# A message pass over 400,000 edges: a ring of 13 chunks for 26, an earlier scatter, and TensorE picks in every second chunk

## What is computed

```python
h = jnp.maximum(_layernorm(x, axis=-1), 0.0)
x_i = h[dst]
x_j = h[src]
feat = jnp.concatenate([x_i, x_j - x_i], axis=-1)
m = jnp.maximum(feat @ W1 + b1, 0.0) @ W2 + b2
out = jax.ops.segment_max(m, dst, num_segments=N)
return x + jnp.where(jnp.isneginf(out), 0.0, out)
```

## Time and profile before

| | us |
|---|---|
| median of 3 runs (4907.32 to 4908.18) | 4908.1 |
| the profiled execution's own time | 4908.0 |
| its span | 4906.2 |
| busy in it: PE / PE's weight loads / DVE / ACT / POOL | 3227.3 / 1841.1 / 2427.4 / 893.1 / 3047.4 |
| the gathers of L386: number, busy | 2865, 2724.1 |
| the picks of L659: number recorded, busy | 9360, 2333.0 |

### The profile page before, as it was taken

One profiled execution on the slowest core, in us unless ns is written; L12 is line 12 of the kernel. 1 busy time (PEld: TensorE's weight loads), 2 busy tenths in 40 slices (PEclk: granted clock), 3 DMA queues, 4 the chain that ended last, 5 costly groups with the idle time before them and its releaser, 6 DMA issues.

```text
span 4906.2 us, 47353 instructions
## 1 busy us (share of the span) xinstructions
PE 3227.3 (66%) x14485; PEld 1841.1 (38%) x14745; DVE 2427.4 (49%) x7621; ACT 893.1 (18%) x3287; POOL 3047.4 (62%) x3186
## 2 busy tenths in 40 slices
PE   2100027777777777777777777777777777778960
PEld 2100004444444444444444444444444444444540
DVE  4100106555555555555555555555555555556861
ACT  4400202111111111111111111111111111112210
POOL 5677756666666666666666666666666666664017
PEclk8555558888888888888888888888888888888985
DMA  7866402222222222222222222222222222222222
GB/s 276 322 227 227 139 24 74 72 75 72 72 75 71 72 73 70 75 72 71 75 72 71 75 71 73 71 72 75 71 72 75 72 72 73 70 74 72 81 83 54
DMA packets 208533, 451.67 MB, mean 92 GB/s; under 512 B 61389, under 2 KB 64442, under 8 KB 207778
## 3 DMA queue, kind: packets, MB, share of 16 engines
q1 hardware_dynamic: 66703, 225.73, 14.3%
q0 software_dynamic: 103216, 117.29, 11.1%
q10 hardware_dynamic: 38362, 105.62, 5.9%
HBM read 230.84 MB, written 217.71 MB: 91 GB/s over the span
## 4 chain that ended last, share of the span: by engine, by line
another core or an unknown queue 41%; issue 28%; DVE 11%; ACT 9%; PE 6%; POOL 2%; DMA 1%; ACTq 1%; DVEq 0%; POOLq 0%; SPq 0%
ACT dst_all L535 5%; PE ps_g L659 5%; DVE state L896 4%; DVE a_fill L869 4%; POOL a_rows L443 2%; DVE rows L882 2%; ACT zt L547 1%; ACT dst_all L526 1%; ACTq L554 1%; DMA shared<-in_x_dram 1%; PE ps_m L678 1%; ACT zt L461 1%; ACT shared L568 0%; ACT shared L488 0%
## 5 line engine op out<-in xcount | busy, mean ns | idle before, releaser
L386 POOL DMA_INDIRECT rows<-b_table,src_idx x2865 | 2724.1, 951 | 1456.8 <-issue 804.3
L659 PE MATMUL ps_g<-shared,dst_all 128*128 128x512 bf16 x9360 | 2333.0, 403 | 255.7 <-issue 251.2
L659 PEld LDWEIGHTS ps_g<-shared,dst_all 128*128 128x128 bf16 x9620 | 1003.0, 105 | 1394.9 <-issue 509.7
L678 PE MATMUL ps_m<-w_diag,zt 128*128 128x128 f32 x3126 | 681.0, 399 | 726.0 <-ACT zt L547 722.5
L678 PEld LDWEIGHTS ps_m<-w_diag,zt 128*128 128x128 f32 x3126 | 611.1, 296 | 901.1 <-ACT zt L547 893.3
L896 DVE SCALAR_TENSOR_TENSOR state<-state,keep,ps_m 128x64 f32<-128x64 f32 x3125 | 859.8, 275 | 73.5 <-PE ps_m L678 43.1
L869 DVE SCALAR_TENSOR_TENSOR a_fill<-a_fill,keep 128x64 f32<-128x64 f32 x3125 | 874.0, 280 | 19.2
L924 DVE TENSOR_TENSOR dst_all<-ps_s,page_keys 128x1664 bf16<-128x1664 f32 x130 | 245.8, 1891 | 894.9 <-remote 890.4
L924 DVE TENSOR_TENSOR dst_all<-ps_x,page_keys 128x1664 bf16<-128x1664 f32 x130 | 245.8, 1891 | 847.9 <-remote 847.9
L547 ACT ACTIVATE zt<-ps_t 128x512 f32<-128x512 f32 (+1 forms) x521 | 226.6, 487 | 1688.6 <-remote 1656.4
L535 ACT ACTIVATE dst_all<-ps_g,dst_all 128x64 f32<-128x64 f32 x2080 | 454.7, 347 | 123.9 <-remote 80.5
(11 more groups left out here) (115 smaller groups left out, 556.2 us busy)
## 6 DMA issues: line engine op xcount, KB each, us to landing
a_edges<-state SPq DMA_DIRECT2D x80, 1250.0 KB
a_fill<-a_edges SPq DMA_DIRECT2D x260, 384.0 KB
states<-state ACTq DMA_DIRECT2D x260, 384.0 KB
rows<-b_table,src_idx POOLq DMA_INDIRECT x2865
shared<-in_x_dram SPq DMA_DIRECT2D x5, 625.0 KB
b_table<-shared ACTq DMA_DIRECT2D x5, 625.0 KB
a_table<-a_rows SPq DMA_DIRECT2D x1, 3125.0 KB
shared<-in_x_dram SPq DMA_DIRECT2D x1, 3125.0 KB
```

The lines of the kernel that those rows point to most:

```text
L386: nc.gpsimd.indirect_dma_start(out=rows[:, c % RING, t * C:(t + 1) * C], out_offset=None, in_=b_table, in_offset=at(src_idx[:, q % SRC_RIN ...
L659: last = nc.tensor.matmul(ps_g[:, half, :], key_is[:, half, g, :], table[:, g, t, :], start=(g, t) == (0, 0), stop=g == PAGES - 1)
L678: last = nc.tensor.matmul(ps_m[:, g, a * C:(a + m) * C], zt[0:m * C, g, a * C:a * C + P], w2_pair[0:m * C, 0:m * C], start=True, stop=True)
```

## The change

- The ring of `rows` has 13 chunks (RING). The search's blocks and the squares, which borrowed room in it, get tiles of their own.
- Picks are made only in chunks 4, 6, 8, ... 258 (EVERY, `picks_in`), 128 in all. The other 132 chunks gather all their 12 tiles. Keys, matches, picks, masks and sums are numbered by pick (`pick_number`) and left out in the other chunks. `gathered_count` gives the semaphore's value that a chunk's gathers end with.
- The 80 clears stand in a straight row and four are in flight (ZQ), each with its own semaphore.
- The store of a_table and the loads of the pages move from SP's queue to ACT's, the first two pages ahead of ACT's last `count_blocks`, the others each behind the split of the page two before.
- POOL gathers 10 chunks (PREFIX, 117 gathers) ahead of the scatters, not 25, and chunks 10 to 12 (34 gathers) behind them; the waits for z_turned begin with chunk 13.
- DVE's wait for the clears and the small gather stands behind the first matches instead of ahead of all of them. `first_dst` is a copy, so that the small gather doesn't read dst_all.
- ACT presets the maxima (one activation) behind step 5 instead of ahead of step 0.

The diff, cut to its core (asserts, new tiles and renamed arguments are left out):

```diff
-    RING = 26
+    RING = 13
...
+    ZQ = 4
...
-    GATHERED = CHUNK - 1
+    PRESET_AT = 5
+    PREFIX = 10
+    EVERY, FIRST_PICK = 2, PICK_AHEAD + 1
+
+    def picks_in(c):
+        return FIRST_PICK <= c < CHUNKS and (c - FIRST_PICK) % EVERY == 0
+
+    def pick_number(c):
+        return (c - FIRST_PICK) // EVERY
+
+    def picks_below(c):
+        return -(-max(0, min(c, CHUNKS) - FIRST_PICK) // EVERY)
+
+    def gathered_tiles(c):
+        return (CHUNK - 1 if picks_in(c) else CHUNK) if c < CHUNKS else TAIL
+
+    def gathered_count(c):
+        return 16 * sum(gathered_tiles(d) for d in range(c % RING, c + 1, RING))
...
+            for z in range(ZEROS):
+                if z >= ZQ:
+                    sp.wait_ge(zeros_stored[z % ZQ], 16 * (z // ZQ))
+                sp.dma_start(a_lanes[:, z * ZW * ZREP:(z + 1) * ZW * ZREP].rearrange("p (r w) -> p r w", w=ZW),
+                             zero_row).then_inc(zeros_stored[z % ZQ], 16)
...
-            def gather_chunk(c, tiles=GATHERED, done=None):
+            def gather_chunk(c, done=None):
                 q, j = divmod(c, BATCHED)
                 if j == 0:
                     pool.wait_ge(src_loaded[q % SRC_RING], (q // SRC_RING + 1) * 16)
-                for t in range(tiles):
+                for t in range(gathered_tiles(c)):
...
-            for c in range(RING - 1):
-                if c == BLOCKS_AT:
-                    pool.wait_ge(blk_used, SEARCHES)
+            for c in range(PREFIX):
                 gather_chunk(c)
             pool.wait_ge(scatter_ready, 1)
-            for half in range(2):
-                pool.wait_ge(zeros_stored[half], 16 * ZEROS // 2)
+            for s in range(ZQ):
+                pool.wait_ge(zeros_stored[s], 16 * ZEROS // ZQ)
...
             scatter_a(BATCH, NJ)
-            gather_chunk(RING - 1)
+            for c in range(PREFIX, RING):
+                gather_chunk(c)
             for c in range(RING, CHUNKS + 1):
                 pool.wait_ge(z_turned, (c - RING + 1) * GROUPS)
...
+            act.wait_ge(a_ready, NJ // 4)
+            act.dma_start(a_nodes, a_rows[0:NP, :, :]).then_inc(a_stored, 16)
+            act.wait_ge(b_stored, 16 * PIECES)
+            act.wait_ge(page_left, 1)
+            for g in range(2):
+                load_page(g)
             count_blocks(SEARCHES)
...
+                if g + 2 < PAGES:
+                    act.wait_ge(page_part, (g + 1) * PARTS)
+                    load_page(g + 2)
...
-                if c + KEYS_AHEAD < CHUNKS:
-                    spread_keys(c + KEYS_AHEAD, k + KEYS_AHEAD)
+                if picks_in(c + KEYS_AHEAD):
+                    spread_keys(c + KEYS_AHEAD)
...
+                if c == PRESET_AT:
+                    act.wait_ge(a_scattered, 16 * NJ)
...
-                if c + PICK_AHEAD < CHUNKS:
-                    pick(c + PICK_AHEAD, k + PICK_AHEAD, range(PAGES_FIRST))
+                if picks_in(c + PICK_AHEAD):
+                    pick(c + PICK_AHEAD, range(PAGES_FIRST))
...
-                if c + MATCH_AHEAD < CHUNKS:
+                if picks_in(c + MATCH_AHEAD):
```

More of the change, by code:

```diff
@@ L178, in edge_conv @@
         zero_row_set = sem("zero_row_set")
[L179 removed]
+        zeros_stored = [sem(f"zeros_stored{s}") for s in range(ZQ)]
         w2_cleared = sem("w2_cleared")
@@ L295, in _ @@
             sp.wait_ge(zero_row_set, 1)
[L296 to L312, removed]
-                for top in range(0, PARTS * QUARTER, QUARTER) if g == PAGES - 1 else (0,):
-                    sp.dma_start(page[top:top + full, g % 2, :], part).then_inc(page_loaded[g % 2], 16)
-                    if rest:
-                        sp.dma_start(page[top + full:top + full + 1, g % 2, 0:rest * C],
-                                     b_table[N - rest:N, :].rearrange("(o e) c -> o (e c)", o=1)
-                                     ).then_inc(page_loaded[g % 2], 16)
-            for half in range(2):
[L321 to L324, removed]
-            sp.wait_ge(a_ready, NJ // 4)
-            sp.dma_start(a_nodes, a_rows[0:NP, :, :]).then_inc(a_stored, 16)
-            for g in range(PAGES):
-                load_page(g)
-            for half in range(2):
-                sp.wait_ge(zeros_stored[half], 16 * ZEROS // 2)
+            for z in range(ZEROS):
[4 more added lines that the diff above has]
+            for s in range(ZQ):
+                sp.wait_ge(zeros_stored[s], 16 * ZEROS // ZQ)
             sp.wait_ge(a_scattered, 16 * NJ)
@@ L502, in _, with load_page @@
             deviation(PIECES - 1)
+            def load_page(g):
+                first_row = g * OCTET * P
+                full = min(P, (N - first_row) // OCTET)
+                part = b_table[first_row:first_row + full * OCTET, :].rearrange("(l e) c -> l (e c)", e=OCTET)
+                rest = (N - first_row) % OCTET if full < P else 0
+                for top in range(0, PARTS * QUARTER, QUARTER) if g == PAGES - 1 else (0,):
+                    act.dma_start(page[top:top + full, g % 2, :], part).then_inc(page_loaded[g % 2], 16)
+                    if rest:
+                        act.dma_start(page[top + full:top + full + 1, g % 2, 0:rest * C],
+                                      b_table[N - rest:N, :].rearrange("(o e) c -> o (e c)", o=1)
+                                      ).then_inc(page_loaded[g % 2], 16)
             for g in range(NJ // 4 + 1):
@@ L944, in fill_all @@
                     fill(c, t)
-            choose(0)
+            for s in range(ZQ):
+                dve.wait_ge(zeros_stored[s], 16 * ZEROS // ZQ)
+            nc.vector.memset(state[:, 1, W - C:W], -FLT_MAX).then_inc(carry_set, 1)
+            dve.wait_ge(ends_gathered, 16)
+            dve.wait_ge(carry_set, 1)
             fill_all(0)
             add(0)
-            choose(1)
             fill_all(1)
```

118 lines of the change are left out of this document (58 added, 60 removed).

## The result

The changed kernel takes 5155.5 us (median of 4, 5152.6 to 5163.7) against 4907.7 us before (median of 4). The ratio is 1.0509, with a 95% interval of 1.0491 to 1.0527: slower by 5.1%. The forecast was 4969 us, slower by 1.2%. The profiled execution, the slowest of the four, took 5163.7 us with a span of 5161.9.

The account below looks back on a forecast made before the run. Bound by the number of indirect DMAs and of pauses, with PE, DVE and ACT in their shadow: 382 (start) + 4173 (2981 DMAs) + 164 (pauses) + 90 (drain) + 158 (end) = 4967 us span, 4969 us time; range 4800 to 5160.

Parts of the forecast that it names:

- Start: Before the first scatter: four clears in flight finish the zeros at about 382 us, 162 us sooner.
- The late rate: Clears before the first scatter: four in flight bring back 349 to 379 GB/s, against 243 with two.
- Number of DMAs: POOL behind the clears: 2981 indirect DMAs against 2691, 290 more at 1.40 us each, +406 us.
- Pauses: POOL's waits for z_turned: 248 × 0.66 = 164 us, or one doubled pause per two chunks at the same cost.
- Rival D: Chunk pairs: POOL drains before PE finishes picks and transposes, idling 2.2 to 4.4 us; 5160 to 5430 us; chance 0.16.
- Drain and end: After the last gathers: 90 us for the ring's 12 or 13 chunks, then an unchanged 158 us.
- A: POOL's waits: one pause of 0.66 us for two chunks, 82 us less, 4887 us; chance 0.20.
- B: POOL's waits: none, because the ring of 13 is deep enough; 4805 us; chance 0.08.
- C: POOL's gathers: 1.40 us is PE's picks' share of a common resource; POOL runs at 1.25, 4440 to 4520; chance 0.06.
- Rival E: Clears at the start: four in flight go only halfway to the high rate, +80 us on any case.
- A slowing of POOL by DVE's matches: POOL's DMA issues beside DVE's matches (L924): halving matches would save up to 249 us if true; forecast gave nothing.

## Why the prediction was right and wrong

The direction was right, and so was the view of the kernel on the chip of the measurement: the count of indirect DMAs at 1.40 us and the pauses set the time. The size was not: +61 us forecast, +248 measured. 5155.5 lies just inside the range's upper end, 5160.

**Start.** Forecast 382 for the first scatter, measured 412.6. +31 us. The late rate was right (380 GB/s), but the sum gave all of it to 52 clears, 65 MB. From 207 to 412 us the chip moved 77.3 MB at 377 GB/s: one clear more (27, not 28, were issued by 207), what was still under way at 207, and 7.1 MB of gathers, pages and the like. 12.3 MB at that rate are 33 us. That the prefix lies under the clears was right; that POOL then stands idle for 76 us was in the sum only through the late start. A longer prefix would have filled some of it, at most with the 34 gathers of chunks 10 to 12, some 43 us, as the ring has no more room.

**Number of DMAs.** 2997 gathers and 290 more DMAs behind the clears, as forecast. The scatters took 1.29 us each, not 1.40 (−11 us). Before, they stood behind 275 gathers without a pause and now behind 76 us of idling; that this is the reason was not tested.

**Pauses: the step that failed.** The term "248 × 0.66 = 164 us" took either a pause per chunk, or one per pair of twice that length. The pair was the right unit: 126 waits. But the timeline has 16 pairs from 3029.53 to 3586.98, 34.84 us each, and 34.84 − 23 × 1.40 = 2.64 us of pause where 1.32 were in the sum. 124 pairs × 1.32 = **+164 us**, the bulk of the miss. What the term left out is the work that PE still has to do when the gathers have been served. In the run's pairs of 23 gathers the 24 whose wait is put down to "remote" take 33.2 us in the mean, a pause of 1.0; the 95 whose wait is put down to PE's transposes take 35.4, a pause of 3.2, and up to 38.5.

Rival D named this mechanism and its price (half of the 16 picks and the transposes still to do when POOL has drained, 2.2 us, 5160 us), with a chance of 0.16 only. What I gave too little weight was already in the trace of before: the earlier trace rows shows picks at one in 2.8 us while PE has many of them waiting and POOL's DMAs are served, and one release for two chunks gives PE 23 gathers in which to run into that.

The clock was in no term either. D took PE's pace from the end of the run, at full clock. By my estimate from the trace, PE has 2.9 picks and 4.3 transposes left in the mean when the 23 gathers are served (by 1.40 each), and they take 0.48 and 0.23 us each, against 0.21 and 0.14 in the kernel before. At that pace they would be done some 1.2 us sooner per pair. So most of the 1.32 us may be the lower clock and not the amount of work left; no run tells the two apart.

D's remark on the 64 places of PE's queue (the Trainium skill, TensorE: Matmul & The Clock Gate, table of specifications) fits in kind. In the pair above 12 + 6 + 21 + 12 + 1 + 6 = 58 matmuls with their loads, 116 entries, run smoothly behind the release, and the crawl sets in then; in the next pair it sets in after 52 matmuls, 104 entries. Both are more than one fill of 64, so some 40 to 50 would have to come through first. And the 112 entries of a cycle before passed without a crawl, so a count from the release is not the whole rule. No run here varied it, and why PE crawls stays open.

**Drain and end.** From the last gather at 4904.7 to L423 at 5013.15:

```profile
5013.15 0.94 POOL L423 DMA_INDIRECT head<-states,lane_i  x1 [107.49 <-DMA states<-state]
```

107.5 us against 99 forecast (90 and the 9 of the last states), and 149 us from there on, as before. +8 us. PE, DVE and ACT all idle for more than half of the run, as forecast; what POOL waits for in the pairs is PE's late transposes all the same.

Sum: +31 − 11 + 164 + 8 = 192, and the profiled span is 195 us over the forecast 4967.

**Rivals A, B, C.** A had its unit right and its price wrong: its 32.9 us per pair is nearly met by the 24 pairs of 33.2, and by no others in the mean. B and C did not happen where the prediction was measured. C's number is another matter: "a gather at 1.25, POOL never waits" is what free chips do, in all the changed kernels traced there and, by the sum, in the kernel before, and then the change costs 266 us as well. So both kinds agree on the sign, for partly different reasons. Had the change been measured on a free chip, the forecast of 1.2% would have met 6.5%. Rival E did not happen. A slowing of POOL by DVE's matches, for which the sum had no term, was small on free chips: 790 to 794 gathers per 1000 us with a match in every chunk, 794 to 796 with every second, 796 to 798 with none. On holding chips no run varied it alone.

## What to carry to other kernels

Where POOL's indirect DMAs are the longest queue, a pick on another engine that replaces one of them is worth the DMA's whole time (1.26 us here on free chips), even if that engine looks busy; giving such picks up to unload PE or DVE bought nothing, because they were in the shadow. Count what stands between two releases on each engine's queue, not the mean load: on holding chips the pattern of a heavy and an empty step went with one release for two chunks, and POOL waited for PE's rest of work. Price such a rest at the clock that the engine will have by then. And fill a wait for clears with gathers up to its end: shortening the wait and the filling together gave POOL 76 to 104 us of idling. Before a comparison, run the old kernel on the same chip: here its own time moved by a factor of 1.2.

## What the runs showed of the hardware

- The same program took 4871 to 4908 us on three occasions and 4074 to 4076 us on five others (four chips), a factor of 1.2 in the whole, with no difference inside either group over 1%. In the first group other engines saw a finished matmul only after 7.1 us of idling (before) and 21.8 us (changed kernel), while indirect DMAs were in service; in the second POOL issued one per 1.26 us without a pause, and the changed kernel has no wait for "remote" there at all.
- In the first group PE itself slows, after 104 to 116 entries behind a release, to one pick matmul in 1.4 to 2.8 us (3043.76 to 3059.21 above), while POOL's DMAs are served.
- With four clears of 1.25 MB in flight, from a straight list, the chip moved 380 GB/s in all, and 243 GB/s with two in flight from a loop, both beside gathers.
